# A macaron block on one core: the buffer for projected query and key chunks in attention gets four places in place of two

## What is computed

```python
def rotate_half(t):
    x1, x2 = jnp.split(t, 2, axis=-1)
    return jnp.concatenate((-x2, x1), axis=-1)
...
qkv = x @ W_qkv                       # 2 sequences of 2048 tokens, 256 wide; 16 heads of 64
q, k, v = jnp.split(qkv, 3, axis=-1)
...
apply_rope = lambda t: t * cos + rotate_half(t) * sin
q, k = (apply_rope(q), apply_rope(k))
dots = jnp.einsum('bhid,bhjd->bhij', q, k) * scale
dots = jnp.where(causal, neg, dots)
attn = jax.nn.softmax(dots, axis=-1)
out = jnp.einsum('bhij,bhjd->bhid', attn, v)
```

## Time and profile before

| what | value |
|---|---|
| median of 3 runs | 5067.33 us (5065.14 to 5069.31) |
| the profiled execution's own time | 5057.61 us |
| its span in the profile | 5056.0 us |
| attention's pipeline in it | from about 2615 to about 4550 us after the start |
| PE, DVE, ACT, POOL busy, share of the span | 73%, 73%, 51%, 47% |
| mean granted clock of TensorE | 0.859 of full speed |

### The profile page before, as it was taken

The page is one execution under the profiler, slowest core; times in us unless marked ns, Lnnn a source line. Parts: engine busy times, 40 slices in busy tenths (PEclk is TensorE's granted clock), DMA queues, the critical chain, the costliest instruction groups (busy, mean ns, idle before and its releaser), DMA issues. The chain is left out here.

```text
span 5056.0 us, 84627 instructions
## 1 busy us (share of the span) xinstructions
PE 3693.8 (73%) x28905; PEld 2609.3 (52%) x28907; DVE 3705.1 (73%) x4463; ACT 2569.0 (51%) x4134; POOL 2388.5 (47%) x1532
## 2 busy tenths in 40 slices
PE   2997645555555569948936898989989899894595
PEld 1663224444444446637813566666656566663484
DVE  6883489999999988840067888888888888885101
ACT  1222456666666632222313677777767676684221
POOL 0220268888888842221034665655656666600202
PEclk9998777777676779959957999999999999996697
DMA  2000001000000100024532222222222222202255
GB/s 86 0 0 4 7 21 32 30 29 29 29 31 30 30 29 0 0 91 146 175 113 58 57 51 52 48 47 68 53 64 54 50 54 52 55 10 92 73 182 155
DMA packets 236313, 276.22 MB, mean 55 GB/s; under 512 B 63820, under 2 KB 183557, under 8 KB 234561
## 3 DMA queue, kind: packets, MB, share of 16 engines
q1 hardware_dynamic: 223056, 244.85, 17.7%
q0 software_dynamic: 8704, 24.35, 1.4%
q10 hardware_dynamic: 4224, 2.76, 0.3%
HBM read 152.60 MB, written 36.04 MB: 37 GB/s over the span
## 5 line engine op out<-in xcount | busy, mean ns | idle before, releaser
L2242 DVE TENSOR_TENSOR att_b_prob_low<-att_b_prob,att_b_prob_high 128x1024 f16<-128x1024 f32 (+2 forms) x640 | 783.7, 1225 | 54.5 <-ACT att_b_prob_high L2209 49.0
L2269 DVE TENSOR_REDUCE att_b_neg_max<-att_b_peek 128x1 f32<-128x1024 f32 (+1 forms) x748 | 667.0, 905 | 143.3 <-PE att_b_peek L2097 114.0
L2207 ACT ACTIVATE att_b_prob<-att_b_score,att_soft 128x1024 f32<-128x1024 f32 (+2 forms) x640 | 633.0, 989 | 223.7 <-PE att_b_score L2120 148.0
L1025 PE MATMUL mix_scan_hT<-ident,mix_scan_h 128*128 128x128 f32 x1024 | 253.3, 395 | 526.6 <-DVE mix_scan_h L973 498.6
L2209 ACT ACTIVATE att_b_prob_high<-att_b_score,att_soft 128x1024 f16<-128x1024 f32 (+2 forms) x640 | 630.1, 985 | 10.2 <-PE att_b_o L2148 3.5
L1025 PEld LDWEIGHTS mix_scan_hT<-ident,mix_scan_h 128*128 128x128 f32 x1024 | 176.5, 200 | 640.7 <-DVE mix_scan_h L973 445.1
L2144 PE MATMUL att_b_o<-att_b_vh,att_b_prob_high 128*128 128x65 f16 x4352 | 463.1, 195 | 37.2 <-DVE att_b_prob_low L2242 26.5
L2118 PE MATMUL att_b_score<-att_b_q_both,att_b_k_twice 128*128 128x512 f16 (+3 forms) x1280 | 448.9, 351 | 28.6 <-ACT att_b_prob_high L2209 18.3
L2144 PEld LDWEIGHTS att_b_o<-att_b_vh,att_b_prob_high 128*128 128x128 f16 x4352 | 401.4, 98 | 130.4 <-DVE att_b_prob_low L2242 71.5
L2148 PE MATMUL att_b_o<-att_b_vh,att_b_prob_low 128*128 128x65 f16 x4352 | 461.8, 194 | 0.0
L2146 PE MATMUL att_b_o<-att_b_vl,att_b_prob_high 128*128 128x64 f16 x4352 | 461.4, 193 | 0.0
(11 more groups left out here) (343 smaller groups left out, 9606.0 us busy)
## 6 DMA issues: line engine op xcount, KB each, us to landing
moe_w<-in_L_ffn_W_dram SPq DMA_DIRECT2D x64, 1024.0 KB, 8.2
mix_scan_b_row<-mix_b_rows SPq DMA_DIRECT2D x128, 256.0 KB, 3.1
att_b_crossed<-att_b_raw SPq DMA_DIRECT2D x512, 64.0 KB, 2.0
att_b_q_both<-att_b_halves SPq DMA_DIRECT2D x240, 64.0 KB, 2.0
att_b_k_twice<-att_b_halves SPq DMA_DIRECT2D x240, 64.0 KB, 2.0
moe_slots_in<-moe_route_zero SPq DMA_DIRECT2D x2, 4096.0 KB, 14.3
moe_exp_x<-moe_slots_in SPq DMA_DIRECT2D x32, 256.0 KB, 4.5
moe_slots_out<-moe_exp_y POOLq DMA_DIRECT2D x32, 256.0 KB, 6.4
```

The costliest lines, as they stand in the source:

```text
L1025: last = pe.transpose(hT_ps[:, j * D + m * P:j * D + (m + 1) * P], hs[:, b * W + m * GRP + t * P:b * W + m * GRP + (t + 1) * P], ident[:, :])
L2207: act.activation(prob[:, at:at + width], score[m % 2][:, 0:width], ACT.Exp, scale=soft[:, 0:1])
L2242: dve.tensor_tensor(prob_low[:, at:at + width], prob[:, at:at + width], prob_high[:, at:at + width], ALU.subtract).then_inc(low_ready, 1)
L2269: last = dve.tensor_reduce(neg_max[:, first + col:first + col + 1], peek_bank(kind, s)[:, base:base + nb * P], AX.X, ALU.max, negate=True)
```

## The change

`raw` becomes four places of 512 columns (`RAWS = 4`); job i uses place i % 4. `crossed` and `halves` keep two. ACT's copy of job i now waits for the rotation of job i-4 where it waited for that of job i-2. That wait had also kept `crossed` from being overwritten, so SP's `cross` gets a wait of its own: the swap of job i waits until the rotation of job i-2 is done.

```diff
+        RAWS = 4
...
-        raw, crossed = sb("raw", [P, 2 * GRP]), sb("crossed", [P, 2 * GRP])
+        raw, crossed = sb("raw", [P, RAWS * GRP]), sb("crossed", [P, 2 * GRP])
...
         def rotate(eng, c, t, i, kind):
...
-            ring = slice(r * GRP, (r + 1) * GRP)
+            ring, mine = slice(r * GRP, (r + 1) * GRP), slice(i % RAWS * GRP, (i % RAWS + 1) * GRP)
...
-            eng.tensor_tensor(raw[:, ring], raw[:, ring], cos[:, at], ALU.mult).then_inc(rope_step, 1)
+            eng.tensor_tensor(raw[:, mine], raw[:, mine], cos[:, at], ALU.mult).then_inc(rope_step, 1)
...
-            c.link(eng.tensor_tensor(raw[:, ring], raw[:, ring], crossed[:, ring], ALU.add), (tables, 32))
+            c.link(eng.tensor_tensor(raw[:, mine], raw[:, mine], crossed[:, ring], ALU.add), (tables, 32))
...
-            c.link(eng.tensor_scalar(high(r), raw[:, ring], 1.0, None, ALU.mult))
-            eng.tensor_tensor(low16(r), raw[:, ring], high(r), ALU.subtract).then_inc(roped, 1)
+            c.link(eng.tensor_scalar(high(r), raw[:, mine], 1.0, None, ALU.mult))
+            eng.tensor_tensor(low16(r), raw[:, mine], high(r), ALU.subtract).then_inc(roped, 1)
...
             def cross(t, i):
-                ring = slice(i % 2 * GRP, (i % 2 + 1) * GRP)
-                sp.wait_ge(raw_ready, qk_count(t + 1, i + 1))
+                ring, mine = slice(i % 2 * GRP, (i % 2 + 1) * GRP), slice(i % RAWS * GRP, (i % RAWS + 1) * GRP)
+                copied, turned = qk_count(t + 1, i + 1), qk_count(t + 1, i - 1)
+                if not isinstance(t, int):
+                    copied, turned = sp.to_reg(copied), sp.to_reg(turned)
+                sp.wait_ge(raw_ready, copied)
+                wait_unless_first(sp, roped, turned)
                 for to, fro in ((0, 32), (32, 0), (64, 96), (96, 64)):
-                    sp.dma_start(crossed[to:to + 32, ring], raw[fro:fro + 32, ring])\
+                    sp.dma_start(crossed[to:to + 32, ring], raw[fro:fro + 32, mine])\
                         .then_inc(crossed_over[i % 2], 16)
...
                 if what == "qk":
-                    r = i % 2
+                    r = i % RAWS
                     act.wait_ge(qk_projected, qk_count(p, i + 1))
-                    wait_unless_first(act, roped, qk_count(p, i - 1))
+                    wait_unless_first(act, roped, qk_count(p, i - RAWS + 1))
                     act.copy(raw[:, r * GRP:(r + 1) * GRP], side_ps[:, :]).then_inc(raw_ready, 1)
```

## The result

Over 15 runs each, the changed kernel took 5074.07 us (5065.94 to 5080.67) and the kernel before 5065.14 us; the ratio is 1.0020, with a 95% interval from 1.0014 to 1.0027. The interval lies above 1: a small slowdown, and not no change. The profiled execution after has a span of 5064.3 us, 8.3 us more than before. The forecast was 5068 us in a range of 5056 to 5084. In what follows one execution of e2 (5131.6 us, at a lower granted clock, 0.820) is left out of e2's median and ratio.

A forecast was written before the change was run, and what follows sets the result against it. POOL's rotations, ending last before step 22's peek, were taken as the bound. Freed waits 0, SP's wait +0.9 and denser DVE 0 gave +1 us, 5058.5 us for the profiled execution, 5068 us for the runs, range 5056 to 5084.

The forecast's parts named there:

- The wait goes and its worth on the path is 0: ACT's copies to `raw`: about 148 us of waiting for POOL practically disappears, worth 0 us on the path.
- The stall at step 18: PE's peek at key chunk 1: a first stall appears there, some 3 to 5 us.
- The stall at step 22: PE's peek at key chunk 2: the 5.4 us wait grows to some 8 to 11.5 us in each turn.
- PE is there 3 to 6 us earlier: PE's way from step 18 to step 22: 11.2 us included ACT waits, so it reaches the stall earlier.
- SP's new wait: SP's `cross`: always met, so only register moves cost, +0.9 us, with bounds of 0 and +7 us.
- POOL beside a denser DVE: Rotations 0 to 5: the DVE work beside them stays the same, so 0 us, bounds -8 to +52 us.
- Rival 3: End of rotation 5: denser DVE work without pauses delays it 1 to 3.5 us per turn, 5082 to 5120 us; chance 0.14.
- Rivals 1, 2 and 4: Waits on path, 4998 us, chance 0.04; rotations 4, 5 quieter, 5046 to 5060, 0.14; copies still wait, 5067, 0.02.
- rival 1: ACT's copies: their waits are on the path after all, so PE's stall ends earlier, 4998 us; chance 0.04.
- POOL shows idle time before one of rotations 1 to 6: Sign of being wrong on POOL's row: rotations 0 to 5 were to take 53 us, still without gaps.
- Rotations 1 to 6 find their input there already: POOL's rotations: no gap that an earlier copy could fill, so the freed waits are worth 0 us.
- attention didn't end where it did: Sign (d), in the changed kernel's profile: attention as a whole was to end where it did before.

The follow-up runs named there:

- e2: The changed kernel without SP's new wait and its register instructions in `cross`; ratio 1.0011 (0.9998 to 1.0024) to the kernel before, 5067.15 us.
- e7: The kernel before, two places, without the multiplication by sine in POOL's rotation (output changes); ratio 0.9728, 4926.60 us.
- e5: The changed kernel, but copy 4 alone waits for the rotation of job i-2 as before; ratio 1.0007 (0.9998 to 1.0016), 5068.16 us.
- e1: The changed kernel, but ACT's copies still wait for the rotation of job i-2; ratio 1.0000 (0.9987 to 1.0012), 5061.32 us.
- e3: The kernel before, two places, with a key chunk's high half stacked early and head 0's peek waiting for two DMAs, not six; ratio 0.9854, 4984.10 us.
- e11: The changed kernel with high halves stacked early, head 0's peek awaiting two DMAs, and copy 4 alone waiting for job i-2 again; ratio 0.9873, 5013.72 us.
- e4: The changed kernel, four places, with high halves stacked early and head 0's peek waiting for two DMAs, not six; ratio 0.9957, 5038.61 us.

## Why the prediction was right, and where it was not

- **The number.** 5068 us stands on the 5067.3 of the first three runs; over 15 runs the kernel before took 5065.14. As a change, +1 us was forecast and +8.9 measured. "No change that can be measured" is not what came out: the interval is clear of 1. That it stayed so near is in part luck: rotation 3 lost 1.4 us per turn, and rotations 4 and 5 happened to give back 1.0.
- **The wait goes and its worth on the path is 0.** Right. ACT's 148.2 us went, e7 shows that the way through POOL is what the turn waits for, and e5, which frees 112 of the 148 us, gains nothing.
- **The stall at step 18.** Right: 3.2 to 3.7 us in most turns, 3 to 5 predicted.
- **The stall at step 22 was to grow to 8 to 11.5 us.** Wrong: 3.7 to 4.4 us in 11 of the 15 turns, and PE's waits at the peek sum to 115 us, not 170 to 240. The step that failed is "PE is there 3 to 6 us earlier". From the peek at 3235.02 to the beginning of the stall, 3251.27 - 3.79 = 3247.48, it took 12.5 us, more than the 11.2 before, though ACT's waits for POOL are gone from it. The window of the changed kernel across the stall at step 18 has the clock at 0.75:

```profile
3231.00:3236.00 5.00, 1.79 (x28) 1.18 (x28) 2.19 (x4) 1.85 (x2) 4.77 (x4) 0.75 0.48 104
```

  From step 18's peek to the next stall (3235.02 to 3247.48) it is 0.79, and PE is busy for 11.99 of 12.46 us with 121 matmuls. Before, in the same stretch (3232.86 to 3244.10), it was 1.00, and PE did the same 121 in 9.82 us. So PE itself set the pace there; ACT waited for it (5.58 us before copy 6).
  The prediction had allowed for a drop at step 18 and taken it out of the spare time, but not out of the stall that it forecast. Since POOL set the end, the error cost nothing.
- **SP's new wait, +0.9 us, at most +7.** Within what e1 and e2 allow: e1, which has it, is level with the kernel before.
- **POOL beside a denser DVE, 0 us.** This is the term that was mis-sized: +0.63 us in rotations 0 to 5 and 0.70 us at step 22 in each turn, some 10 us, inside the bounds of -8 to +52. The argument was that the work of DVE beside the rotations stays the same, so the blocking does too. The amount did nearly stay (19.1 low parts start within rotations 0 to 5 before, 18.4 after, means of the 15 turns), but who blocks whom did not: a pause of DVE lets POOL's operation start first, and then DVE pays; without the pause POOL pays. DVE's busy time fell from 3705.1 to 3681.0 us, POOL's rose from 2388.5 to 2396.3. The prediction's sentence behind its citation, that by the lock's rule the total of the blocking stays, leaves the same thing out: by that rule the one that starts second pays, and here the order changed. Of the 10 us, 3.0 are the two gaps before rotation 5.
- **Rival 3** named this mechanism, its place, and the very pause before 3221.70. It set the lowest price at 1 us per turn, and 0.7 as the point from which it decides; the measured value lies on that point, as a mean; only three of the 15 turns are over it, the first and the two with the gap before rotation 5. So the case that happened stands between the forecast and rival 3, on the boundary of 0.2%.
- **Rivals 1, 2 and 4** are out: nothing was gained, rotations 4 and 5 did get quieter, by 0.6 and 0.4 us, but rotation 3 took more than that, and the change did what it says. In the Trainium skill (Perfetto Trace Analysis, "Optimization Strategy") the sentence that rival 1 rests on is about the engine that should be saturated. In rotations 0 to 5 that is not ACT, which is busy for 37.71 of 53.20 us, but POOL with 50.66.
- **The signs of being wrong.** "POOL shows idle time before one of rotations 1 to 6" came true, in five turns: 1.28 and 1.73 us before rotation 5, 0.4 to 0.6 before rotation 6. The step behind it, "Rotations 1 to 6 find their input there already", failed there: rotation 5 waits where rotation 4 took only 7.8 us. And attention didn't end where it did: the last turn began 8.7 us later, at 4361.61.

## What to carry to other kernels

The waits that a deeper buffer removes are worth something only if the time isn't given back later. Here all of them stood ahead of a place where everything waits for POOL's last piece, and there what counts is the way through POOL and on to the first operation that needs its result. Look there for the DMAs and the semaphore counts that are waited for needlessly: waiting for two of six DMAs and starting on the first half was worth 1.5% here. And where the engine that sets the time and a busy one block each other, an idle wait of the busy one may be what lets the other through.

## What the runs showed of the hardware

- A GpSimd operation of two SBUF inputs, 128x512 float32, 1.26 us free, took 2.18 to 2.25 us beside a VectorE operation of two SBUF inputs (1.21 us free) that had started first; the other way round the VectorE operation took 2.16 us.
- Stalls of PE of 1.6 us left the granted clock at 1.00 behind them in the windows shown or named (e3, e11); behind stalls of 3.2 us it was 0.73 (e11), behind 5.4 us 0.54 and behind 6.8 us 0.55 (e4).
